# Bu products copied to bf16 by ScalarE before the rotation and scan on VectorE

## The reference

```python
x = L0_attn_inputs                       # 8 x 8192 x 1024, float32
xn = _layernorm(x, axis=-1)
# recurrence, with Lambda = exp(-exp(nu_log) + 1j*exp(theta_log))
Bu = einsum('ph,blh->blp', (B_re + 1j*B_im) * gamma[:, None], xn)
xs[t] = Lambda * xs[t-1] + Bu[t]         # written as an associative scan
s  = einsum('hp,blp->blh', C_re + 1j*C_im, xs).real + D * xn
# FFN
h  = relu(xn @ W1 + b1)                  # 1024 -> 4096
g  = silu(h @ W2 + b2)                   # 4096 -> 1024
return x + s * g
```

## Time and profile before

| | |
|---|---|
| median of 3 runs | 4081.38 us (4081.2 to 4151.98) |
| the profiled execution | 4074.66 us |
| span of its slowest core | 4073.6 us |
| spans of its cores | 4049.4 to 4073.6 us |
| granted PE clock, mean of the cores | 0.880 to 0.883 |

### The profile page before, as it was taken

One profiled execution on the slowest core, in us unless ns is written; L12 is line 12 of the kernel. 1 busy time (PEld: TensorE's weight loads), 2 busy tenths in 40 slices (PEclk: granted clock), 3 DMA queues, 4 the chain that ended last, 5 costly groups with the idle time before them and its releaser, 6 DMA issues.

```text
span 4073.6 us, 61096 instructions; the slowest of 8 cores (4049.4 to 4073.6 us)
## 1 busy us (share of the span) xinstructions
PE 3099.7 (76%) x21760; PEld 2237.6 (55%) x21760; DVE 2225.5 (55%) x3641; ACT 983.7 (24%) x1894; POOL 22.0 (1%) x46
## 2 busy tenths in 40 slices
PE   2401579797987879797887879797887979797898
PEld 1201256473856656483755657483755657383767
DVE  5770084655738284655838384655828384665501
ACT  3102212221322313221322312222322312122322
POOL 0010000000000000000000000000000000000000
PEclk9855689898998989898998989898998989898999
DMA  5775457393846747383756748383756748394776
GB/s 139 190 150 147 139 167 247 128 288 122 258 156 221 234 153 261 116 287 135 240 174 216 233 144 276 107 288 134 243 181 209 233 144 282 105 288 141 232 235 221
DMA packets 409225, 800.90 MB, mean 197 GB/s; under 512 B 50528, under 2 KB 50528, under 8 KB 406880
## 3 DMA queue, kind: packets, MB, share of 16 engines
q1 hardware_dynamic: 361184, 738.26, 55.6%
q10 hardware_dynamic: 41984, 41.95, 3.0%
q0 software_dynamic: 5760, 16.78, 2.8%
HBM read 755.01 MB, written 58.72 MB: 200 GB/s over the span
## 4 chain that ended last, share of the span: by engine, by line
PE 58%; DVE 23%; DMA 6%; ACT 6%; issue 5%; DVEq 1%; ACTq 1%; SPq 0%; POOL 0%; POOLq 0%
PE PB L752 23%; PE PB L555 11%; PE PA L792 10%; PE PB L792 8%; DMA h<-W 4%; DVE s_b L823 3%; DVE g_b L837 2%; PE PB L674 2%; DVE vv L693 2%; DVE vv L699 2%; DVE g_b L692 2%; DVE tmp L690 2%; DVE g_b L698 2%; DVE tmp L696 2%; PE PB L417 2%
## 5 line engine op out<-in xcount | busy, mean ns | idle before, releaser
L752 PE MATMUL PB<-xnf,wslot 128*128 128x256 bf16 x8192 | 980.7, 286 | 247.6 <-DVE vv L699 244.8
L752 PEld LDWEIGHTS PB<-xnf,wslot 128*128 128x128 bf16 x8192 | 838.3, 103 | 392.1 <-issue 260.9
L762 ACT ACTIVATE h<-PB,b_tab 128x256 bf16<-128x256 f32 x1024 | 485.8, 474 | 1439.0 <-PE PB L752 1412.0
L823 DVE SCALAR_TENSOR_TENSOR s_b<-xnf,d_tab,s_b 128x256 f32<-128x256 bf16 x256 | 124.1, 485 | 694.7 <-ACT g_b L806 670.7
L792 PE MATMUL PA<-h,wslot 128*128 128x256 bf16 x4096 | 468.0, 273 | 45.7 <-ACT h L762 44.7
L792 PE MATMUL PB<-h,wslot 128*128 128x256 bf16 x4096 | 468.1, 273 | 0.0
L792 PEld LDWEIGHTS PA<-h,wslot 128*128 128x128 bf16 x4096 | 398.3, 98 | 99.8 <-issue 54.0
L792 PEld LDWEIGHTS PB<-h,wslot 128*128 128x128 bf16 x4096 | 400.8, 98 | 46.3
L674 PE MATMUL PA<-xnf,wslot 128*128 128x512 bf16 x1024 | 266.0, 422 | 107.4 <-DVE vv L699 107.4
L417 PE MATMUL PB<-ident,s_b 128*128 128x128 f32 x256 | 62.1, 424 | 300.0 <-ACT s_b L409 205.8
L674 PE MATMUL PB<-xnf,wslot 128*128 128x512 bf16 x1024 | 243.7, 399 | 54.7 <-DMA wslot<-sc_b 27.6
(11 more groups left out here) (87 smaller groups left out, 2592.4 us busy)
## 6 DMA issues: line engine op xcount, KB each, us to landing
wslot<-sc_w SPq DMA_DIRECT2D x256, 2048.0 KB, 10.5
wslot<-sc_b SPq DMA_DIRECT2D x32, 2048.0 KB, 10.3
wslot<-sc_c SPq DMA_DIRECT2D x32, 2048.0 KB, 10.9
xsl<-x SPq DMA_DIRECT2D x32, 1024.0 KB, 5.7
out<-xsl ACTq DMA_DIRECT2D x32, 1024.0 KB, 4.8
h<-W POOLq DMA_DIRECT2D x8, 1024.0 KB, 13.7
sc_w<-h SPq DMA_DIRECT2D x8, 1024.0 KB, 8.1
h<-W POOLq DMA_DIRECT2D x32, 256.0 KB, 4.7
```

The lines of the kernel that those rows point to most:

```text
L752: inst = nc.tensor.matmul(bank[:, 0:256], pslot(jw)[:, kk * 1024 + ml * 128: kk * 1024 + (ml + 1) * 128], xnf_p[:, kk * NSUP + sub * NSUB: ...
L762: ev = S(lambda m2=mi, b=bank: nc.scalar.activation(h1[:, m2 * NSUB:(m2 + 1) * NSUB], b[:, 0:256], AF.Relu, bias=b1_tab[:, m2:m2 + 1]))
L823: nc.vector.scalar_tensor_tensor(s_b[:, m2 * NSUP + sub * NSUB: m2 * NSUP + sub * NSUB + NSUB], xnf_p[:, m2 * NSUP + sub * NSUB: m2 * NSUP ...
```

## The change

Between Bu's PSUM and the vector chain there is now a copy: ACT moves the 1024 columns of block m to `vv[m]`, in bf16 (`bu_evac[m]`), and there are eight such buffers instead of three of f32. DVE waits for ACT, not PE. PE takes the banks again when ACT has emptied them. ACT waits for the end of the last step's work on the same `vv[m]` (`rest_last_prev`).

The six operations ahead of the scans take their scratch in `xsre`, `xsim` and `vv[m]`, all bf16. Four of them read bf16 and an f32 table and write bf16; the last two have bf16 only. The scans read bf16 and write f32, in `tmp0` and in `g_b`. In the forward rotation four operations read f32 and write bf16, two have bf16 only.

`emit_rot` no longer uses `vv[0]` and works in halves of 256 columns, with twice as many operations. `xn_tok` becomes bf16, and its 16 transposes of a step are matmuls with a bf16 identity `identb` as the moving operand; those of `g_b` stay f32. For the first chain it is now ACT that waits for the stores from `xsre`.

```diff
-    vv = [sb(f"vv{i}", [128, 2 * NSUP], F32) for i in range(3)]
+    vv = [sb(f"vv{i}", [128, 2 * NSUP], BF16) for i in range(CH)]
...
-    xn_tok = sb("xn_tok", [128, 2 * H], F32)
+    xn_tok = sb("xn_tok", [128, 2 * H], BF16)
...
+    identb = sb("identb", [128, 128], BF16)
...
     def emit_rot(kk):
         if kk == 0:
             return
-        rt = vv[0][:, 0:NSUP]
+        t_a = tmp0[:, 0:NSUB]
+        t_b = tmp0[:, NSUB:2 * NSUB]
         for m in range(CH):
-            cseg = cS[:, m * NSUP:(m + 1) * NSUP]
-            sseg = sS[:, m * NSUP:(m + 1) * NSUP]
-            V(lambda a=tmp[0][:, :], b=sseg, s2=sD[:, m:m + 1]:
-              nc.vector.tensor_scalar(a, b, s2, None, ALU.mult))
-            V(lambda a=rt, b=cseg, s2=sD[:, m:m + 1]:
-              nc.vector.tensor_scalar(a, b, s2, None, ALU.mult))
-            V(lambda a=cseg, s2=cD[:, m:m + 1]:
-              nc.vector.scalar_tensor_tensor(
-                  a, a, s2, tmp[0][:, :], ALU.mult, ALU.subtract))
-            V(lambda a=sseg, s2=cD[:, m:m + 1]:
-              nc.vector.scalar_tensor_tensor(
-                  a, a, s2, rt, ALU.mult, ALU.add))
+            for hf in range(2):
+                off = m * NSUP + hf * NSUB
+                cseg = cS[:, off:off + NSUB]
+                sseg = sS[:, off:off + NSUB]
+                V(lambda a=t_a, b=sseg, s2=sD[:, m:m + 1]:
+                  nc.vector.tensor_scalar(a, b, s2, None, ALU.mult))
+                V(lambda a=t_b, b=cseg, s2=sD[:, m:m + 1]:
+                  nc.vector.tensor_scalar(a, b, s2, None, ALU.mult))
+                V(lambda a=cseg, s2=cD[:, m:m + 1], t=t_a:
+                  nc.vector.scalar_tensor_tensor(
+                      a, a, s2, t, ALU.mult, ALU.subtract))
+                V(lambda a=sseg, s2=cD[:, m:m + 1], t=t_b:
+                  nc.vector.scalar_tensor_tensor(
+                      a, a, s2, t, ALU.mult, ALU.add))
...
     VX(GP)
+    V(lambda: nc.vector.tensor_copy(identb[:, :], ident[:, :]))
+    m_identb = VE.n
...
+            if k == 0:
+                TX(VE, m_identb)
             for sub in range(2):
-                src_tok = xn_tok if sub == 0 else g_b
...
-                        inst = nc.tensor.transpose(
-                            PB[:, bk * 512 + tbl * 128:
-                               bk * 512 + tbl * 128 + 128],
-                            src_tok[:, (tb % 2) * H + c * 128:
+                        dst = PB[:, bk * 512 + tbl * 128:
+                                 bk * 512 + tbl * 128 + 128]
+                        if sub == 0:
+                            inst = nc.tensor.matmul(
+                                dst,
+                                xn_tok[:, (tb % 2) * H + c * 128:
+                                       (tb % 2) * H + (c + 1) * 128],
+                                identb[:, :], start=True, stop=True)
+                        else:
+                            inst = nc.tensor.transpose(
+                                dst,
+                                g_b[:, (tb % 2) * H + c * 128:
                                     (tb % 2) * H + (c + 1) * 128],
-                            ident[:, :])
+                                ident[:, :])
...
             if st_first_chain:
-                VX(BST[0])
-                VX(BST[1])
+                SX(BST[0])
+                SX(BST[1])
                 st_first_chain = False
-            vmul_mark = [0] * CH
+            bu_evac = [0] * CH
+            rest_last = [0] * CH
 
             def emit_rest(m):
                 cseg = cS[:, m * NSUP:(m + 1) * NSUP]
                 sseg = sS[:, m * NSUP:(m + 1) * NSUP]
-                vrr = vv[m % 3][:, 0:NSUP]
-                vii = vv[m % 3][:, NSUP:2 * NSUP]
+                vrr = vv[m][:, 0:NSUP]
+                vii = vv[m][:, NSUP:2 * NSUP]
+                yr = tmp[0][:, :]
...
-                V(lambda a=vrr, d0=rb, d1=vrb, mm=m:
...
-                V(lambda a=vii, d0=rb2, d1=vib, mm=m:
...
-                V(lambda mm=m, a=vrr: nc.vector.tensor_copy(
+                V(lambda mm=m, a=yr: nc.vector.tensor_copy(
                     carry[:, 2 * mm:2 * mm + 1], a[:, NSUP - 1:NSUP]))
-                V(lambda mm=m, a=vii: nc.vector.tensor_copy(
+                V(lambda mm=m, a=yi: nc.vector.tensor_copy(
                     carry[:, 2 * mm + 1:2 * mm + 2], a[:, NSUP - 1:NSUP]))
                 xr = xsre[:, m * NSUP:(m + 1) * NSUP]
                 xi2 = xsim[:, m * NSUP:(m + 1) * NSUP]
-                V(lambda a=tmp[0][:, :], b=cseg, c2=vrr:
+                V(lambda a=xr, b=cseg, c2=yr:
                   nc.vector.tensor_tensor(a, b, c2, ALU.mult))
-                V(lambda a=tmp[1][:, :], b=sseg, c2=vii:
+                V(lambda a=vrr, b=sseg, c2=yi:
                   nc.vector.tensor_tensor(a, b, c2, ALU.mult))
-                V(lambda a=xr: nc.vector.tensor_tensor(
-                    a, tmp[0][:, :], tmp[1][:, :], ALU.subtract))
-                V(lambda a=tmp[0][:, :], b=sseg, c2=vrr:
+                V(lambda a=xr, b=vrr: nc.vector.tensor_tensor(
+                    a, a, b, ALU.subtract))
+                V(lambda a=vrr, b=sseg, c2=yr:
                   nc.vector.tensor_tensor(a, b, c2, ALU.mult))
-                V(lambda a=tmp[1][:, :], b=cseg, c2=vii:
+                V(lambda a=vii, b=cseg, c2=yi:
                   nc.vector.tensor_tensor(a, b, c2, ALU.mult))
-                V(lambda a=xi2: nc.vector.tensor_tensor(
-                    a, tmp[0][:, :], tmp[1][:, :], ALU.add))
+                rest_last[m] = V(lambda a=xi2, b=vrr, c2=vii:
+                                 nc.vector.tensor_tensor(a, b, c2, ALU.add))
...
                 if m >= 4:
-                    TX(VE, vmul_mark[m - 4])
+                    TX(SE, bu_evac[m - 4])
...
                 last_bu = TE.inc(inst)
 
+                SX(TE, last_bu)
+                SX(VE, rest_last_prev[m])
+                bu_evac[m] = S(lambda mm=m, p=pt, b=base:
+                               nc.scalar.activation(
+                                   vv[mm][:, :], p[:, b:b + 1024],
+                                   AF.Identity))
-                ur = pt[:, base:base + 512]
-                ui = pt[:, base + 512:base + 1024]
-                vrr = vv[m % 3][:, 0:NSUP]
-                vii = vv[m % 3][:, NSUP:2 * NSUP]
-                VX(TE, last_bu)
-                V(lambda a=tmp[0][:, :], b=cseg, c2=ur:
+                ur = vv[m][:, 0:NSUP]
+                ui = vv[m][:, NSUP:2 * NSUP]
+                xr = xsre[:, m * NSUP:(m + 1) * NSUP]
+                xi2 = xsim[:, m * NSUP:(m + 1) * NSUP]
+                VX(SE, bu_evac[m])
+                V(lambda a=xr, b=ur, c2=cseg:
                   nc.vector.tensor_tensor(a, b, c2, ALU.mult))
-                V(lambda a=tmp[1][:, :], b=sseg, c2=ui:
+                V(lambda a=xi2, b=ur, c2=sseg:
                   nc.vector.tensor_tensor(a, b, c2, ALU.mult))
-                V(lambda a=vrr: nc.vector.tensor_tensor(
-                    a, tmp[0][:, :], tmp[1][:, :], ALU.add))
-                V(lambda a=tmp[0][:, :], b=cseg, c2=ui:
+                V(lambda a=ur, b=ui, c2=sseg:
                   nc.vector.tensor_tensor(a, b, c2, ALU.mult))
-                V(lambda a=tmp[1][:, :], b=sseg, c2=ur:
-                  nc.vector.tensor_tensor(a, b, c2, ALU.mult))
-                vmul_mark[m] = V(lambda a=vii: nc.vector.tensor_tensor(
-                    a, tmp[0][:, :], tmp[1][:, :], ALU.subtract))
+                V(lambda a=ui, c2=cseg:
+                  nc.vector.tensor_tensor(a, a, c2, ALU.mult))
+                V(lambda a=ur, b=xr: nc.vector.tensor_tensor(
+                    a, b, a, ALU.add))
+                V(lambda a=ui, b=xi2: nc.vector.tensor_tensor(
+                    a, a, b, ALU.subtract))
                 if m >= 2:
                     emit_rest(m - 2)
...
-            vmul_mark_prev = vmul_mark
+            rest_last_prev = list(rest_last)
+            bu_evac_prev = bu_evac
...
-            pp_release(bu_pp[0], "VE", vmul_mark[4])
-            pp_release(bu_pp[1], "VE", vmul_mark[4])
-            pp_release(bu_pp[2], "VE", vmul_mark[5])
-            pp_release(bu_pp[3], "VE", vmul_mark[5])
+            pp_release(bu_pp[0], "SE", bu_evac[4])
+            pp_release(bu_pp[1], "SE", bu_evac[4])
+            pp_release(bu_pp[2], "SE", bu_evac[5])
+            pp_release(bu_pp[3], "SE", bu_evac[5])
...
-                TX(VE, vmul_mark_prev[6])
-                TX(VE, vmul_mark_prev[7])
+                TX(SE, bu_evac_prev[6])
+                TX(SE, bu_evac_prev[7])
                 TX(SE, h1_ev_last)
```

More of the change, by code:

```diff
@@ L70, in build_program @@
     if DEBUG:
-        for nm, shp, dt in [("dbg_xn", [128, 2048], F32),
+        for nm, shp, dt in [("dbg_xn", [128, 2048], BF16),
                             ("dbg_xnf", [128, 4096], BF16),
@@ L279, in build_program @@
     st_first_chain = True
+    rest_last_prev = [0] * CH
+    bu_evac_prev = [0] * CH
     st_first_ffn = True
```

(10 more changed lines are left out.)

## The result

| | before | after |
|---|---|---|
| the profiled execution | 4074.66 us | 3934.59 us |
| span of its slowest core | 4073.6 us | 3933.5 us |
| ratio after / before | 1 | 0.9628, 95% interval 0.9601 to 0.9654 |

The kernel became 3.7% faster. By the ratio, 4081.38 us become 3929.5; the forecast was 3966. By the profiled executions 140 us are gone, of which the forecast's sum has 115. The ratios leave out executions in which half of the chip ran over 1% longer at a lower granted clock, but in some of the rest a few cores did too, so a ratio and the quotient of two profiled executions (0.9656 here) differ by some tenths of a per cent.

A forecast was written before the change was run, and what follows sets the result against it. PSUM release stalls PE, and the vector chain is nearly as long. A step gains 8.3 - 1.2 + 1.3 = 8.4 us; 15 steps give 126, less 11 for the clock is 115: 3966 us, range 3925 to 4015.

The forecast's parts named there:

- Which path sets the end: Before Silu: PE's stalls at L674 and L752 go, about 18 us of waiting appears before the transposes, the chain decides.
- the chain is late next: Bu to Silu: 27.6 us of PE stalls count only until the vector chain is late, since Silu waits for it.
- The fast operations: Vector chain: four all-bf16 operations a block fall from 692 to 425 ns, eight mixed stay; 8.3 us a step saved.
- The scans: Vector chain, two a block: left at their time with bf16 in.
- Rival E: Vector chain: mixed operations and scans pay for bf16 beside f32; at 0.25 us each 4266 us; chance 0.05.
- The copy: ACT's evacuation of Bu's PSUM: 1.02 us plus 0.15 handover, so DVE starts 1.2 us later a step.
- Behind the chain: Chain's end to L823: Silu no longer waits for PE, 3.8 us instead of 5.1, saving 1.3 a step.
- Hidden work: Rotation in halves, 33.9 us against 23.2, lies under sub 1's W1/W2; DMA waits fit in 12 us of PE slack.
- The clock at Bu's start: PE before Bu: faster bf16 transposes leave it idler, four more steps start cold at 2.8 us each, costing 11 us.

The follow-up runs named there:

- the full-width kernel: The changed kernel with the table rotation in 512 columns again, second scratch in `vv[0]`; ratio to before 0.9639 (0.9621 to 0.9658).
- the shortest chain: The changed kernel with bf16 tables and scan outputs, so all twelve tensor_tensor of a block are bf16 only; ratio to before 0.9038, profiled 3708.9 us.

## Why the prediction was right, and where its sizes were off

The forecast was 3966 us, range 3925 to 4015; the measured time is 3929.5 by the ratio, in the range and 4.5 us above its low end. The mechanism held. That the range held with two terms off by 8 and 13 us in the same direction, both below, is in part luck. By its steps:

- **Which path sets the end.** Right. The stalls turned into one wait at the transposes, "about 18 us": 18.8 us in the mean, 19.76 in the row above. The copy alone gains 0.4% at most by either measure, as the step "the chain is late next" says.
- **The fast operations.** Taken at 425 ns between bounds of 167 and 692: measured 425. The eight mixed ones taken at 692: measured 692. The chain, 94.6 forecast, is 94.46. The rule of the Trainium skill ("VectorE: DVE Perf Modes", "What auto-detection actually checks") agrees with both kinds here, and the page's cycle formula gave 424 ns.
- **The scans** with bf16 in: 1283 as before. Rival E has no ground.
- **The copy.** 1.02 us forecast and measured, 1.19 with its handover (3152.85 to 3154.04 on the timeline).
- **Behind the chain.** 3.8 us forecast, 3.85 measured. The gain was sized by step 14's 5.1; the mean of the steps is 5.37. That is 0.2 us a step, 3 us.
- **Hidden work.** The rotation (33.9 us forecast; 64 operations, 353 and 485 ns) is hidden, shown by the full-width kernel. The DMA wait at W1 was put at 4 to 6.5 us a step and is 2.3 (36 in 16 in the mean of the cores). So PE's slack is 17, not 12 us. Neither was in the sum.
- **The clock at Bu's start.** This term failed. I put 11 us for faster transposes that leave PE idler. With f32 transposes nothing changes. The chain's start moved by 1.40 us, of which the copy is 1.19; the rest, 0.2 a step, is 3 us in all, 8 less than forecast. The count I started from was that of one core, on the reasoning that one core's trace speaks for all: six slow starts of 15 on the slowest. Over the eight cores the first 32 matmuls of Bu take over 7.5 us in 28 of 120 starts, 3.5 of 15, and by core in one to six. In the kernel after it is 52 of 120, 6.5 of 15. So there are three more slow starts, not far from my four, but they are short: in steps 1 to 14 a slow one delays the chain by 1.7 us against a fast one, before by 2.3, and the length of nearly 10 us that I priced at 2.8 comes 17 times before and twice after. What makes more of the starts slow is open. It is neither the type of the transposes (49 of 112 with both) nor the copy alone: with the fast operations and no copy, on six cores, 68 of 84 are slow.
- **Left out of the sum.** I held everything from the Silu tail to the next Bu unchanged. It is 0.85 us a step shorter, 13 us, nearly all in W1 of sub 1 (31.38 to 30.60 us). Open: see below.

Together 3 + 8 + 13, and 1 from the chain, make the 25 us between 115 and 140.

**What stays open.** W1 of sub 1 is the same 256 matmuls in both. Its length varies from step to step, between 30.0 and 31.7 us, with the clock in its first 7 us. Two windows of the kernel after (length, busy PE PEld DVE ACT POOL, PEclk, DMA share, GB/s), of a step in which it takes 30.06 us and one in which it takes 31.28:

```profile
1276.90:1284.00 7.10, 7.10 (x62) 6.17 (x60) 5.74 (x13) 2.95 (x7) 0.00 (x0) 0.92 0.39 149
3261.10:3268.20 7.10, 7.10 (x52) 5.70 (x50) 5.76 (x13) 2.37 (x5) 0.00 (x0) 0.76 0.47 158
```

The kernel before has both kinds as well, 0.93 and 29.99 us in one step, 0.71 and 31.57 in another, but more of the second. Why the change shifts the share is open. The longer stand of PE ahead of it is no explanation: in the kernel with the fast operations but without the copy, PE stands there as it did before (1.4 and 2.6 us), and W1 takes 30.47 us. With the copy alone, where it stands longest, it takes 31.03. Nor is it the transposes, whose f32 form leaves 30.58. By period it is 30.81 at 204 us, 30.60 and, with the rotation in full width, 30.70 at 220, 30.99 at 223, 30.47 at 225, 31.03 and 31.38 at 229, which is no clear order either.

## What to carry to other kernels

Before valuing a stall, measure the second path to the next meeting point: here 22 us of PE stall a step were worth 0.4% or less alone, since the vector chain ended 1.5 us before PE's work. Here the copy out of PSUM paid only together with the fast operations, and the narrow type paid only in the tensor_tensor operations in which every operand is narrow; one f32 table kept an operation at its full 692 ns. When the bound has moved, pad the engine that lost it with known work: what disappears is its slack, and that bounds the next gain. And read a count or a wait on all cores before comparing two kernels: between cores of one execution the DMA wait at W1 went from 23 to 59 us.

## What the hardware showed that I had not expected

- The granted clock at the start of Bu did not depend on whether the 16 transposes ahead of it were f32 (351 ns in the mean) or bf16 (256 ns): the chain starts 5.70 and 5.71 us behind Bu, and 49 of 112 starts are slow in both.
- The scan takes 1283 to 1284 ns for 512 columns with the data f32 in and out, bf16 in, or bf16 in and out. The decay `r_tab` is f32 in all three, so no run shows a scan with bf16 only. At this price the scans are 2 x 8 x 1.39 = 22 of the 77.8 us of the shortest chain.
- A tensor_scalar from bf16 to f32 takes 487 ns for 512 columns, as from f32 to f32. So for tensor_scalar and tensor_tensor alike (692 ns) mixed types cost what f32 costs; one with bf16 only is in the runs for tensor_tensor alone.
